# The token phase rebuilt: sums of squares on ScalarE, rows scaled in PSUM, wide low parts, routing in four pieces, folding by subtraction

## What is computed

```
x = x + L0_conv(ln_c(x))          # batch norm, sign, grouped 3x3 convolution, batch norm, residual, PReLU
t = tokens(x)                     # 16384 tokens of 128 channels
t = t + moe0(ln_t(t))             # 8 experts, the best 2 of each token
x = x + L1_conv(ln_c(x))          # an involution
t = t + moe1(ln_t(tokens(x)))     # 16 experts
```

```
ln_t(v) = (v - mean(v)) / sqrt(var(v) + 1e-5)                  # per token, over its 128 channels
logits  = ln_t(t) @ W_router;  probs = softmax(logits)
topk_p, topk_i = top_k(probs, 2);  topk_p /= topk_p.sum()
out     = sum over the two experts e of  p_e * (relu(xn @ W1[e] + b1[e]) @ W2[e] + b2[e])
```

## Time and profile before

| | us |
|---|---|
| median of 3 runs | 1430.45 (1428.18 to 1431.97) |
| the profiled execution, its time | 1428.51 |
| its span, first to last instruction | 1426.5 |
| busy in the span: TensorE / VectorE / ScalarE / GpSimd | 1141.3 / 893.0 / 705.8 / 543.8 |

### The profile page before, as it was taken

One profiled execution on the slowest core, in us unless ns is written; L12 is line 12 of the kernel. 1 busy time (PEld: TensorE's weight loads), 2 busy tenths in 40 slices (PEclk: granted clock), 3 DMA queues, 4 the chain that ended last, 5 costly groups with the idle time before them and its releaser, 6 DMA issues. The chain is left out here.

```text
span 1426.5 us, 32796 instructions
## 1 busy us (share of the span) xinstructions
PE 1141.3 (80%) x9966; PEld 751.3 (53%) x9967; DVE 893.0 (63%) x2020; ACT 705.8 (49%) x1452; POOL 543.8 (38%) x401
## 2 busy tenths in 40 slices
PE   6869777777474999999999999758887887864586
PEld 2324343443212999999999999723333333322354
DVE  3653477787661555555555555427888888884576
ACT  5855444444212555555555555445545554522364
POOL 0000016556540333333333333327778877881000
PEclk9989888788655999999999999979999999995599
DMA  6100001111411111111111111121111110101000
GB/s 201 44 1 0 1 8 44 41 38 55 163 57 42 45 39 40 39 42 41 38 39 41 41 40 41 33 81 30 30 35 54 59 59 29 45 30 76 0 1 30
DMA packets 60530, 63.21 MB, mean 44 GB/s; under 512 B 9843, under 2 KB 50432, under 8 KB 60467
## 3 DMA queue, kind: packets, MB, share of 16 engines
q1 hardware_dynamic: 49620, 44.45, 10.5%
q0 software_dynamic: 8832, 17.00, 3.6%
q10 hardware_dynamic: 2016, 0.94, 0.2%
HBM read 35.11 MB, written 28.55 MB: 45 GB/s over the span
## 5 line engine op out<-in xcount | busy, mean ns | idle before, releaser
L803 POOL DMA_INDIRECT expert_out<-m_result,m_token x148 | 144.5, 977 | 364.4 <-DVE m_result L935 361.0
L923 DVE SCALAR_TENSOR_TENSOR m_hl<-ps,m_hh 128x512 f16<-128x512 f32 x292 | 200.3, 686 | 106.2 <-ACT m_hh L895 106.2
L895 ACT ACTIVATE m_hh<-ps 128x512 f16<-128x512 f32 x292 | 174.3, 597 | 172.9 <-PE ps L856 170.7
L838 PE MATMUL ps<-m_x,weights 128*128 128x128 f16 x1168 | 212.5, 220 | 10.7 <-issue 2.8
L840 PE MATMUL ps<-m_x,weights 128*128 128x128 f16 x1168 | 211.6, 220 | 0.0
L839 PE MATMUL ps<-m_x,weights 128*128 128x128 f16 x1168 | 211.4, 219 | 0.0
L853 PE MATMUL ps<-weights,m_hh 128*128 128x128 f16 x1160 | 209.2, 219 | 0.0
L855 PE MATMUL ps<-weights,m_hl 128*128 128x128 f16 x1160 | 209.2, 219 | 0.0
L854 PE MATMUL ps<-weights,m_hh 128*128 128x128 f16 x1160 | 209.2, 219 | 0.0
L747 POOL DMA_INDIRECT dispatched<-d_rows,slot x128 | 126.2, 986 | 205.1 <-DVE slot L654 120.9
L1045 POOL TENSOR_TENSOR iv_pool_sum<-iv_pool_sum,iv_pool_part 128x1024 f32<-128x1024 f32 x80 | 188.6, 2357 | 12.9 <-DVE iv_pool_part L1262 4.7
(11 more groups left out here) (318 smaller groups left out, 2320.7 us busy)
## 6 DMA issues: line engine op xcount, KB each, us to landing
m_rows<-dispatched SPq DMA_DIRECT2D x152, 65.5 KB, 1.8
X<-x SPq DMA_DIRECT2D x16, 512.0 KB, 4.3
iv_got<-expert_out SPq DMA_DIRECT2D x16, 512.0 KB, 4.3
out<-X SPq DMA_DIRECT2D x16, 512.0 KB, 3.0
Y<-w_moe SPq DMA_DIRECT2D x8, 512.0 KB
expert_out<-m_result,m_token POOLq DMA_INDIRECT x148, 2.2
dispatched<-d_rows,slot POOLq DMA_INDIRECT x128, 2.4
e_w<-w_moe SPq DMA_DIRECT2D x3, 512.0 KB, 8.0
```

Of the source, the lines that this page charges most:

```text
L803: pool.indirect_dma_start(env.yt, bass.IndirectOffsetOnAxis(ap=token[:, k:k + 1], axis=0), result[:, k, :], None, bounds_check=TOKENS - 1, ...
L838: pe.matmul(out, high, xh, start=True, stop=False)
L895: act.activation(hh[e][:, :], hidden[e], ACT.Relu).then_inc(hi_ready[e], 1)
L923: dve.scalar_tensor_tensor(hl[e][:, :], hidden[e], 0.0, hh[e][:, :], ALU.max, ALU.subtract).then_inc(h_split[e], 1)
```

## The change

In the loop:
- The variance no longer comes from VectorE. ScalarE squares each tile of `turned` with an accumulator output (`square(n)`), which gives the sum of squares of each centered row.
- ScalarE scales all 136 columns of each tile (rows and logits) by 1/sqrt where they lie in PSUM, four instructions per unit, waits for these, and writes the fp16 high part of all four tiles in one instruction.
- VectorE copies the logits and writes the low parts of a unit in one subtraction (`scores(n)`), in place of one product and four instructions.
- The token numbers go to the rows by ScalarE, once per span.
- The routing of a span is spread over the four units that follow it: `choose`, `pair`, `share`, `route` on VectorE, the rank matmuls in two parts (second and third unit) on TensorE. The ranks start from an fp32 product that spreads `seen`, and their 17th column group becomes the new `seen`, so the reduction of `hot` and the matmul for the counts go. TensorE waits for `hot` in the second unit of each span, between mix(n+2) and turn(n+1).
- positive runs two units ahead instead of three; it and keep now follow the squares.

Weights:
- The loads start in the loop, each as soon as the units of Y under it are used; b1 takes the place of the last row of W1 on the host, and a new input `w1_last` (2 MB) holds that row on every partition but the last.
- VectorE subtracts it (`base`), two experts at a time, in the last four units. The fold matmuls go. ScalarE rounds all weights after its last unit, with the last span's Exp between experts 1 and 2; VectorE writes the low parts after the table, and the bias rows last.

The diff, cut to its core:

```diff
-            sp.wait_ge(sum_ready, UNITS)
-            sp.dma_start(b1, a["b1"]).then_inc(w_loaded, 16)
+            for e in range(E0):
+                sp.wait_ge(sum_ready, E0 * 2 + e)
+                sp.dma_start(raw[:, e, :], a["w_moe0"][e, :, :]).then_inc(w_loaded, 16)
+            sp.wait_ge(sum_ready, rest0 // HALF)
+            sp.dma_start(last_row, a["w1_last"]).then_inc(w_loaded, 16)
+            sp.wait_ge(sum_ready, rest0 // HALF + 2)
...
-            sp.dma_start(fold, a["k_fold"]).then_inc(w_loaded, 16)
-            sp.dma_start(only, a["k_only"]).then_inc(w_loaded, 16)
-            for e in range(E0):
-                sp.dma_start(raw[e], a["w_moe0"][e, :, :]).then_inc(w_loaded, 16)
...
                 if n >= 2:
-                    pe.wait_ge(normed, n - 1)
                     pe.wait_ge(taken, n - 1)
...
-            def ranks(c):
-                pe.wait_ge(hot_ready, c + 1)
-                pe.matmul(prefix, env.ltri[:, :], hot[:, :, :].rearrange("p t a -> p (t a)"), start=True, stop=False)
-                if c > 0:
-                    pe.wait_ge(summed, c)
-                    pe.matmul(prefix, env.ones16[:, :], seen[:, :].unsqueeze(1).broadcast_to([P, SPAN, PAIRS]), start=False, stop=False)
-                for t in range(SPAN - 1):
-                    after = SPAN - 1 - t
-                    mm = pe.matmul(prefix[:, (t + 1) * PAIRS:SPAN * PAIRS], env.ones16[:, :],
-                                   hot[:, t:t + 1, :].broadcast_to([P, after, PAIRS]), start=False, stop=(t == SPAN - 2))
-                mm.then_inc(prefix_ready, 1)
+            def ranks(c, part):
+                if part == 0:
+                    pe.wait_ge(summed, c + 1)
+                    pe.matmul(prefix, env.idf[:, :], seen[:, :].unsqueeze(1).broadcast_to([P, SPAN + 1, PAIRS]), start=True, stop=False)
+                    pe.wait_ge(hot_ready, c + 1)
+                    pe.matmul(prefix[:, 0:SPAN * PAIRS], env.ltri[:, :], hot[:, :, :].rearrange("p t a -> p (t a)"), start=False, stop=False)
+                for t in range(0, 6) if part == 0 else range(6, SPAN):
+                    mm = pe.matmul(prefix[:, (t + 1) * PAIRS:(SPAN + 1) * PAIRS], env.ones16[:, :],
+                                   hot[:, t:t + 1, :].broadcast_to([P, SPAN - t, PAIRS]), start=False, stop=(t == SPAN - 1))
+                if part == 1:
+                    mm.then_inc(prefix_ready, 1)
 
...
-                if n % SPAN_UNITS == 0 and n > 0:
-                    ranks(n // SPAN_UNITS - 1)
-            ranks(SPANS - 1)
-            pe.wait_ge(summed, SPANS)
-            pe.matmul(spare[:, 0:PAIRS], env.ones16[:, :], seen[:, :], start=True, stop=True).then_inc(counted, 1)
-            pe.wait_ge(w_loaded, 16 * (E0 + 4))
-            pe.wait_ge(x_ready, UNITS)
-            for e in range(E0):
-                if e >= 2:
-                    pe.wait_ge(low, 2 * e - 2)
-                pe.matmul(mixture[e % 2], fold, raw[e][:, 0:H0], start=True, stop=False)
-                pe.matmul(mixture[e % 2], only, b1[:, e * H0:(e + 1) * H0], start=False, stop=True).then_inc(folded, 1)
-            pe.wait_ge(counted, 2)
+                c, k = n // SPAN_UNITS - 1, n % SPAN_UNITS
+                if c >= 0 and k in (1, 2):
+                    ranks(c, k - 1)
+            ranks(SPANS - 1, 0)
+            ranks(SPANS - 1, 1)
+            pe.wait_ge(counted, 1)
...
+            def square(n):
+                act.wait_ge(rows_ready, n + 1)
+                for j in range(UNIT_TILES):
+                    act.activation(sq[:, j, :], turned[n % 2][:, place(j):place(j) + C], ACT.Square, accum_out=var[:, j:j + 1]).then_inc(sq_ready, 1)
+
             def normalize(n):
-                act.wait_ge(var_ready, n + 1)
-                act.activation(rstd[:, n, :], var[:, :], ACT.Ln, bias=env.eps[:, 1:2], scale=1.0 / C).then_inc(ln_ready, 1)
+                act.wait_ge(sq_ready, (n + 1) * UNIT_TILES)
+                act.activation(rstd[:, :], var[:, :], ACT.Ln, bias=env.eps[:, 1:2], scale=1.0 / C).then_inc(ln_ready, 1)
                 act.wait_ge(ln_ready, n + 1)
-                act.activation(rstd[:, n, :], rstd[:, n, :], ACT.Exp, scale=-0.5).then_inc(rstd_ready, 1)
+                act.activation(rstd[:, :], rstd[:, :], ACT.Exp, scale=-0.5).then_inc(rstd_ready, 1)
                 act.wait_ge(rstd_ready, n + 1)
-                c, first = n // SPAN_UNITS, n % SPAN_UNITS * UNIT_TILES
-                if c >= ROW_SETS:
-                    act.wait_ge(sent[c % ROW_SETS], c // ROW_SETS * SPAN * 16)
                 for j in range(UNIT_TILES):
-                    ins = act.activation(halves[c % ROW_SETS][:, first + j, 0:C], turned[n % 2][:, place(j):place(j) + C], ACT.Copy,
-                                         scale=rstd[:, n, j:j + 1])
-                ins.then_inc(normed, 1)
+                    at = turned[n % 2][:, place(j):place(j) + C + E0]
+                    act.activation(at, at, ACT.Copy, scale=rstd[:, j:j + 1]).then_inc(scaled, 1)
+                c = n // SPAN_UNITS
+                if n % SPAN_UNITS == 0:
+                    if c >= ROW_SETS:
+                        act.wait_ge(sent[c % ROW_SETS], c // ROW_SETS * SPAN * 16)
+                    act.activation(rows[c % ROW_SETS][:, :, C + 2], env.token_no[:, c * SPAN:(c + 1) * SPAN], ACT.Copy)
+                act.wait_ge(scaled, (n + 1) * UNIT_TILES)
+                act.activation(by_bank(rows_of(n)[:, :, 0:C]), tiles_of(n)[:, :, :, 0:C], ACT.Copy).then_inc(normed, 1)
...
+            def round_weights(e):
+                act.wait_ge(based, e // 2 + 1)
+                at = e * WCOLS
+                act.activation(W[:, at:at + H0], raw[:, e, 0:H0], ACT.Copy, scale=WSCALE).then_inc(high, 1)
+                act.activation(W[:, at + 2 * H0:at + 3 * H0], raw[:, e, H0:2 * H0], ACT.Copy, scale=WSCALE).then_inc(high, 1)
+
             positive(0)
             positive(1)
             keep(0)
-            positive(2)
             for n in range(UNITS):
+                square(n)
+                if n + 2 < UNITS:
+                    positive(n + 2)
                 if n + 1 < UNITS:
                     keep(n + 1)
-                if n % SPAN_UNITS == 0 and n > 0:
+                if n % SPAN_UNITS == 1 and n > 1:
                     shares(n // SPAN_UNITS - 1)
-                if n + 3 < UNITS:
-                    positive(n + 3)
                 normalize(n)
+            act.wait_ge(w_loaded, 16 * (E0 + 2))
+            for e in range(2):
+                round_weights(e)
             shares(SPANS - 1)
-            act.wait_ge(w_loaded, 16 * (E0 + 4))
-            for e in range(E0):
-                at = e * WCOLS
-                act.activation(W[:, at + 2 * H0:at + 3 * H0], raw[e][:, H0:2 * H0], ACT.Copy, scale=WSCALE).then_inc(high, 1)
-                act.wait_ge(folded, e + 1)
-                act.activation(W[:, at:at + H0], mixture[e % 2], ACT.Copy, scale=WSCALE).then_inc(high, 1)
+            for e in range(2, E0):
+                round_weights(e)
             pad(act, 1)
...
 
-            def statistics(n):
-                dve.wait_ge(rows_ready, n + 1)
-                if n > 0:
-                    dve.wait_ge(ln_ready, n)
...
-
             def scores(n):
                 first = n % SPAN_UNITS * UNIT_TILES
                 dve.wait_ge(normed, n + 1)
-                dve.tensor_tensor(l[:, first:first + UNIT_TILES, :].rearrange("p (b s) e -> p b s e", b=2), logits(n),
-                                  rstd[:, n, :].rearrange("p (b s) -> p b s", b=2).unsqueeze(3).broadcast_to([P, 2, 2, E0]),
-                                  ALU.mult)
-                for j in range(UNIT_TILES):
-                    at = halves[n // SPAN_UNITS % ROW_SETS][:, first + j, :]
-                    ins = dve.scalar_tensor_tensor(at[:, C:2 * C], turned[n % 2][:, place(j):place(j) + C], rstd[:, n, j:j + 1], at[:, 0:C],
-                                                   ALU.mult, ALU.subtract)
-                ins.then_inc(taken, 1)
+                dve.tensor_copy(by_bank(l[:, first:first + UNIT_TILES, :]), tiles_of(n)[:, :, :, C:C + E0])
+                at = rows_of(n)
+                dve.tensor_tensor(by_bank(at[:, :, C:2 * C]), tiles_of(n)[:, :, :, 0:C], by_bank(at[:, :, 0:C]), ALU.subtract)\
+                   .then_inc(taken, 1)
 
             over_e = lambda x: x.unsqueeze(2).broadcast_to([P, SPAN, E0])
             rev = env.rev.unsqueeze(1).broadcast_to([P, SPAN, E0])
...
+            def route(c):
                 dve.wait_ge(prefix_ready, c + 1)
-                link(dve.tensor_tensor(flat(where), prefix, flat(hot), ALU.mult))
-                dve.tensor_reduce(fresh[:, :], hot[:, :, :].rearrange("p t a -> p a t"), AX.X, ALU.add)
-                link(dve.tensor_reduce(v["rank"], where[:, :, :], AX.X, ALU.add))
+                where = prefix[:, 0:SPAN * PAIRS]
+                link(dve.tensor_tensor(where, where, flat(hot), ALU.mult))
```

(54 more changed lines are left out.)

72 lines of the change are left out of this document (31 added, 41 removed).

## The result

The changed kernel takes **1368.9 us** (median of 4 runs, 1367.7 to 1369.5); the kernel before, on the same chip, 1431.2. The ratio is 0.9565, 95% interval 0.9546 to 0.9585: 62.3 us less. The profiled execution took 1367.7 us with a span of 1365.8.

The account below looks back on a forecast made before the run. Bound: a VectorE-ScalarE relay in the loop, then a tail of folds, roundings and paddings. Spans of 21.5 instead of 27.1 us save 39, the tail 23: 1428.5 - 61.9 = 1366.6, forecast 1367 us, range 1356 to 1376.

Parts of the forecast that it names:

- ScalarE's unit: Loop: squares, positive, keep, Ln and Exp, scalings and the wide copy on ScalarE sum to 4.54 us, taken as 4.55.
- The unit that waits for the one-hot tile: Loop, second unit of a span: tile at 4.2 us, then rank matmuls and the transposing product, 6.5 us in all.
- 0.7 us per span for changes of level: Loop, TensorE: clock level changes of about 2 us each in one span of three, added to 20.8 us.
- has 0.9 us to spare and starts 0.8 us after the slots: GpSimd: 20.6 us of scatters per 21.5 us span leave 0.9; each block starts 0.8 after its slots.
- T: ScalarE's start of unit 31, forecast at 338.4 us; the tail's times are counted from it.
- Last span's scatters: Tail, GpSimd: last 16 scatters take 22.9 us beside VectorE's bias chain and paddings, against 20.6 in the loop's spans.
- Loads, "cost nought": Weight loads started inside the loop cost nothing and cover the ten units after residual(15); without that cover some 10 us.
- C: Rival: GpSimd paces everything; 1361 us at 20.6 a span, 1380 us at 23.0; chance 0.08 at 23.
- A: Rival: TensorE falls back to 1.2 GHz in the two rank units, span 25 us, 1391 us; chance 0.13.
- B: Rival: ScalarE is the bound at 5.7 us a unit, span 23.7 us, 1387 us; chance 0.09.
- D: Rival: slower, TensorE runs the whole loop at 1.2 GHz, 33 us a span, 1457 us; chance 0.04.
- E: Rival: the VectorE-ScalarE relay stays, span near 26 us, little more than the tail's gain, 1398 us; chance 0.06.

Follow-up runs that it names:

- the run of the loop alone: Changed kernel with the old weights handling (folds, b1 row, separate low parts): 1382.8 us against 1430.2 before; on slower chips 1485.1 and 1485.3 us.
- the run with the operands in PSUM: Changed kernel with one input of VectorE's last-row subtractions and low parts moved to PSUM, bias rows left as they were: 1363.7 us.
- the tail alone: Kernel before with only the new handling of the first expert layer's weights, old loop kept: 1460.7 us beside 1485.4.

## Why the prediction was right, point by point

The time (1367 against 1368.9) and the end of the phase (387.9 against 386.8) were right, and that GpSimd ends last was right too. But two terms of the sum were off by 11.3 and 10.4 us and cancelled, so the closeness of the number is in good part luck.

- **ScalarE's unit**: 4.55 forecast, 4.44 to 4.45 measured. A square with its read takes 0.25 to the next (212.53 to 212.78), 0.285 was forecast.
- **The unit that waits for the one-hot tile**: 6.5 forecast, 6.45 measured. The third unit was over-sized: 5.1 forecast, 4.66 measured. Its ten rank matmuls were priced at 1.3 and took 0.84.
- **0.7 us per span for changes of level**: nil in the loop (granted 1.00 from 186 to 328 us). That is 4.9 us over seven spans; the over-sized units are another 0.8 a span, 5.6 us. The other 0.8 lies outside these spans. A span is 20.0 and not 21.5, and ScalarE began unit 31 at 327.1, not 338.4. This is the first step that failed, by 11.3 us.
- **GpSimd**: "has 0.9 us to spare and starts 0.8 us after the slots" was the other step that failed, and follows from the first. With 20.0 us between slots and 20.6 to send them it fell behind from the second span on. The sixth span's scatters began 4.4 us after their slots (310.90), the seventh's 8.8, the last's 19.5. The working "T + 2.6 + 0.8 + 20.6 + 22.9 + 2.4" with the true T gives 376.4; the end was at 386.8. Of the 10.4 us between, 8.0 are the backlog (8.8 instead of 0.8), 2.5 the seventh span's scatters, 2.1 the landing, less 1.9 for the last span's scatters and 0.3 for its slots.
- **Last span's scatters**: 22.9 forecast for it, and 20.6 for those before it. Measured: 22.9 in the sixth (from 315.3), 23.1 in the seventh (from 338.2), 21.0 in the last. Most of the excess stands beside the new subtractions and the low parts, not beside the casts that I had blamed: a cast accounts for one scatter of 1.13.
- **Landing**: 2.6 us from the last scatter's end to the next phase forecast, 4.5 measured.
- **VectorE's end** T + 41 forecast, T + 37.8 measured; **slots** T + 15.7 and T + 14.7; **paddings** off the path, as said.
- **Loads, "cost nought"**: so in the changed kernel. What they cover is 5.8 us of the last slots, by the run of the loop alone, where some 10 were forecast without that cover.
- **39 us in the loop, 23 in the tail**: 47 and 15 by the run of the loop alone.
- **The signs**: spans of 21 to 22 us, named for right, did not come (20.0), nor did a spacing of 0.28 (0.25). GpSimd spans over 22, named for wrong (C), came twice, 22.9 and 23.1. GpSimd's gaps, the clock and its place as the last to end came as named.
- **Rivals**: C, GpSimd pacing everything, is what happened. It was priced at 1361 (20.6 a span) and 1380 (23.0); at the measured 170.3 us for 128 scatters, 21.3 a span, it lies between. C had a chance of 0.08. The forecast and C differed only in which of two close limits set the pace, and a faster loop than forecast moved the bound to GpSimd's at almost the same time. A, B, D and E did not occur on this chip (span 20.0, clock 1.00). On the second kind of chip the gain was as small as E's (28 us, at a span of 31.2), by a mechanism that no row of the kernel before had shown.

## What to carry to other kernels

Ahead of a sum, list the engines that have a floor in the loop and how far below the new pace each lies: here GpSimd's 20.6 us a span capped a loop that came out at 20.0, and once the first slots were there, further work on ScalarE or TensorE could not have shown in the time. Once an engine is the floor, look at what its neighbours do to it: moving an operand of VectorE's instructions to PSUM gave back 4.5 of 131.6 us of scatters without touching them. And measure such a change on more than one chip before calling its gain its own: 62 us here were 28 elsewhere.

## What the runs showed of the hardware

- A scatter of 128 rows takes 0.97 us on GpSimd. If a VectorE instruction whose inputs lie in SBUF has begun before it and is still running, the scatter lasts until 0.84 us after that instruction's end: 1.50 us beside the low parts back to back, 1.57 to 1.91 beside three of the 1.22 us subtractions (tensor_tensor), 1.13 beside a cast, 1.05 to 1.27 beside the residual. A residual that began less than 0.1 us before the scatter, or inside it, left it at 0.97; in the back-to-back low parts a start 0.02 us before the scatter was enough. Instructions with an input in PSUM left it at 0.97.
- A tensor_scalar of 128x1024 in fp32 that began inside a scatter held its end: three scatters (1.01 here, 1.26 in the run with the operands in PSUM, 1.32 in the run of the loop alone) ended 0.12 to 0.13 us after it. No run was made to test this.
- The Trainium skill (SBUF — State Buffer, Who interferes with whom) has tensor_tensor take only the shared pair's read side and infers from this why it did not hold up the generation of descriptors, and counts casts and tensor_scalar among the instructions that can contend with GpSimd. For the last two these traces agree (1.13 beside a cast, 1.01 to 1.32 beside tensor_scalar). A tensor_tensor under way did lengthen the scatters (1.91), so the inference doesn't cover that case; the measurement decides.
- While a load of 2 MB was on its way, GpSimd waited 7.45 us for a scatter's landing; its next such wait was 1.85. That the load is the cause is read from the order of the two, not tested.
- On two of four further chips a step that waits for another instruction came late once in every block of scatters (waits of up to 11.6 us in the changed kernel). ScalarE's 14 paddings, issued late in an unbroken train of scatters, took 38.7 and 38.9 us there instead of 14.9; issued 0.9 us after the start of a block (the tail alone), 14.6. The changed kernel's phase took 63 us longer there, the rest of its program 24. The cause is open.
